# The mixture-of-experts stages: scoring from the layer's own rows, one-hots for several tiles at once, 39 tiles

## The reference, cut to what matters

```python
def _layernorm(x, axis=-1, eps=1e-05):
    m = jnp.mean(x, axis=axis, keepdims=True); v = jnp.var(x, axis=axis, keepdims=True)
    return (x - m) / jnp.sqrt(v + eps)

def _L0_ffn_ref(x, centroids, gamma, beta, W1, b1, W2, b2):      # E = 8 experts, D = 128, F = 512
    def _sublayer(xs, g, b, W1e, b1e, W2e, b2e):
        mu = jnp.mean(xs, axis=-1, keepdims=True)
        var = jnp.mean(jnp.square(xs - mu), axis=-1, keepdims=True)
        h = (xs - mu) * jax.lax.rsqrt(var + EPS) * g + b
        return xs + jax.nn.relu(h @ W1e.T + b1e) @ W2e.T + b2e
    feats = x.reshape(-1, x.shape[-1])
    expert = jnp.argmax(feats @ centroids.T, axis=1)
    alpha = jax.nn.sigmoid(jnp.sum(feats * centroids[expert], axis=-1, keepdims=True))
    ys = jax.vmap(_sublayer, in_axes=(None, 0, 0, 0, 0, 0, 0))(feats, gamma, beta, W1, b1, W2, b2)
    y = jnp.einsum('te,etd->td', jax.nn.one_hot(expert, E), ys)
    return (alpha * y + (1.0 - alpha) * feats).reshape(x.shape)

x = x + _L0_ffn_ref(_layernorm(x), ...)      # twice, an attention layer between
```

## Time and profile before

| | |
|---|---|
| time, median of 3 runs | 2809.09 us |
| profiled execution, its span | 2815.74 us, 2814.2 us |
| busy, share of the span: PE, DVE, ACT, POOL | 76%, 82%, 66%, 59% |
| first expert layer | 573 to 774 us |
| second expert layer | 1150 to 1352 us |

### The profile page before, as it was taken

The page is one execution under the profiler, slowest core; times in us unless marked ns, Lnnn a source line. Parts: engine busy times, 40 slices in busy tenths (PEclk is TensorE's granted clock), DMA queues, the critical chain, the costliest instruction groups (busy, mean ns, idle before and its releaser), DMA issues. The chain is left out here.

```text
span 2814.2 us, 59782 instructions
## 1 busy us (share of the span) xinstructions
PE 2125.2 (76%) x17516; PEld 1786.7 (63%) x17517; DVE 2299.4 (82%) x5649; ACT 1857.1 (66%) x4289; POOL 1659.4 (59%) x1493
## 2 busy tenths in 40 slices
PE   5628888867589999666458887888888537888886
PEld 2226666756578888566346665777777426777776
DVE  6489999864478888633878884999999888999997
ACT  3559999734455555244335555999888438999886
POOL 0179999615400000055456554999999418999996
PEclk9769999969799999689679997999999759999999
DMA  2013333141200000111010000000000000000001
GB/s 57 2 33 98 96 97 96 64 134 40 60 16 0 0 0 1 31 39 43 25 39 2 0 0 1 1 0 0 0 0 0 1 1 1 0 0 0 0 0 30
DMA packets 67864, 70.93 MB, mean 25 GB/s; under 512 B 10328, under 2 KB 46384, under 8 KB 67632
## 3 DMA queue, kind: packets, MB, share of 16 engines
q1 hardware_dynamic: 61488, 57.56, 7.0%
q0 software_dynamic: 5120, 10.50, 1.4%
q10 hardware_dynamic: 1120, 1.22, 0.2%
HBM read 57.45 MB, written 11.80 MB: 25 GB/s over the span
## 5 line engine op out<-in xcount | busy, mean ns | idle before, releaser
L1794 POOL TENSOR_TENSOR k7a_psums<-k7a_sims 128x1024 f32<-128x1024 f32 x224 | 421.8, 1917 | 18.0 <-DVE k7a_w L2002 13.8
L1794 POOL TENSOR_TENSOR k5a_psums<-k5a_sims 128x1024 f32<-128x1024 f32 x224 | 421.8, 1914 | 17.9 <-DVE k5a_w L2002 13.7
L957 POOL TENSOR_TENSOR mc_hc<-mc_h,mc_cs 128x512 f32<-128x512 f32 x256 | 327.7, 1298 | 32.6 <-DVE mc_h L924 16.6
L1859 PE MATMUL k7a_pw<-g_ident,k7a_w 128*128 128x128 f32 x2048 | 265.5, 277 | 72.5 <-DVE k7a_hid L2011 47.9
L1859 PE MATMUL k5a_pw<-g_ident,k5a_w 128*128 128x128 f32 x2048 | 265.5, 277 | 72.3 <-DVE k5a_hid L2011 47.9
L924 DVE TENSOR_TENSOR_SCAN mc_h<-mc_dA,mc_inj 128x512 f32<-128x512 f32 x256 | 298.2, 1199 | 4.0 <-ACT mc_dA L881 4.0
L1859 PEld LDWEIGHTS k7a_pw<-g_ident,k7a_w 128*128 128x128 f32 x2048 | 226.8, 141 | 115.7 <-DVE k7a_w L2002 52.7
L1859 PEld LDWEIGHTS k5a_pw<-g_ident,k5a_w 128*128 128x128 f32 x2048 | 226.8, 141 | 115.5 <-DVE k5a_w L2002 52.5
L2002 DVE SCALAR_TENSOR_TENSOR k7a_w<-k7a_psums,k7a_best,k7a_lift 128x1024 f32<-128x1024 f32 x224 | 279.1, 1270 | 0.5 <-ACT k7a_lift L1930 0.3
L2002 DVE SCALAR_TENSOR_TENSOR k5a_w<-k5a_psums,k5a_best,k5a_lift 128x1024 f32<-128x1024 f32 x224 | 279.1, 1270 | 0.5 <-ACT k5a_lift L1930 0.3
L1930 ACT ACTIVATE k7a_lift<-k7a_psums 128x1024 f32<-128x1024 f32 x224 | 228.4, 1019 | 35.3 <-DVE k7a_w L2002 30.9
(11 more groups left out here) (532 smaller groups left out, 6059.7 us busy)
## 6 DMA issues: line engine op xcount, KB each, us to landing
mc_cs<-c_rows SPq DMA_DIRECT2D x128, 256.0 KB, 3.1
e_w<-in_L_ffn_W_dram SPq DMA_DIRECT2D x16, 256.0 KB, 5.1
token_rows<-e_zn SPq DMA_DIRECT2D x16, 256.0 KB, 3.6
e_zn<-token_out SPq DMA_DIRECT2D x16, 256.0 KB, 5.7
g_X<-in_L_attn_a_x_dram SPq DMA_DIRECT2D x8, 256.0 KB, 6.0
out_dram<-g_X SPq DMA_DIRECT2D x1, 2048.0 KB, 8.7
e_zs<-token_rows,e_token POOLq DMA_INDIRECT x80
token_out<-e_ys,e_token POOLq DMA_INDIRECT x80
```

Source lines behind the costliest of these rows:

```text
L957: nc.gpsimd.tensor_tensor(hc[:, q % RH, :], h_[:, q % RB, :], cs[:, S % RC, :], ALU.mult).then_inc(outs, 1)
L1794: nc.gpsimd.tensor_tensor(psums[:, h - 1, :, :], rows_of(p, h), s2, ALU.add).then_inc(pooled, 1)
L1859: ins = nc.tensor.matmul(pw[:, j, :], w[:, h % WR, j * P:(j + 1) * P], env.ident[:, :], start=(h == 0 and j % 4 == 0), stop=(h == HD - 1 a ...
```

## The change

- Scales: the 17 operations run inside the layer's block. The two square roots stand on ScalarE behind its first and its second copy of transposed rows.
- Scores: TensorE transposes X, not the normalised rows, and does not wait for these; the centroids have their mean subtracted (three VectorE operations), which leaves the order of scores and, times 1/sd, the score itself. In the first layer the rows of centroids, gamma, beta and b1 are loaded, transposed and copied inside the block, ahead of the first score. SP issues these four loads and the 17 of the weights first.
- Normalising: VectorE does six chunks, GpSimd the last two. VectorE waits for the weight loads only after the list is made.
- Maxima are taken from PSUM, without a copy.
- Weight groups: two ahead of the counts (`EARLY`), seven more ahead of the list (`MIDDLE` = 9), the last seven behind it; ScalarE copies them in the same order, with its half of the one-hots in between, and its sigmoid after them.
- One-hots: the tile comparison in two halves, its scaling on ScalarE and GpSimd, half by half; the place comparison in five operations of 8, 8, 8, 4 and 4 tiles, with the places in PSUM; the products wait once for each of the five.
- The loop runs over 39 tiles.
- End: ScalarE writes two chunks to PSUM, which VectorE adds; GpSimd adds the other six; VectorE takes all statistics.

```diff
 TensorE
-                pe.wait_ge(normed, n + 1)
                 need(pe, written, n - 1)
-                    ins = nc.tensor.transpose(pz[...], zn[:, n * TPC + k, :], env.ident[:, :])
+                    ins = nc.tensor.transpose(pz[...], env.X[:, n * TPC + k, :], env.ident[:, :])
                 ins.then_inc(turned, 1)
+                if n == 1 and rows:
+                    pe.wait_ge(centred, 3)
+                    nc.tensor.transpose(counts[:, 0:3 * E], rows3[:, :], env.ident[0:3 * E, 0:3 * E])
+                    nc.tensor.transpose(counts[:, 3 * E:3 * E + E * J], rows1[:, :], ...).then_inc(rows_turned, 1)
+                    pe.wait_ge(rows_out, 2)
...
-            for g in range(EARLY, len(groups)):
+            for g in range(EARLY, min(MIDDLE, len(groups))):
                 turn_group(g)
-            pe.wait_ge(spread, 2)
-            for t in range(NT):
-                pe.wait_ge(compared, t + 1)
-                nc.tensor.matmul(ids[...], hotr[:, t, :], hotq[:, t, :, :], ...).then_inc(found, 1)
+            for i, (t0, t1) in enumerate(GROUPS):        # (0, 8), (8, 16), (16, 24), (24, 28), (28, 32)
+                pe.wait_ge(spread, 1 if t1 <= NT // 2 else 2)
+                pe.wait_ge(spread_p, 1 if t1 <= NT // 2 else 2)
+                pe.wait_ge(compared, i + 1)
+                for t in range(t0, t1):
+                    ins = nc.tensor.matmul(ids[...], hotr[:, t, :], hotq[:, t, :, :], ...)
+            ins.then_inc(found, 1)
+            for g in range(MIDDLE, len(groups)):
+                turn_group(g)
 ScalarE
                 nc.scalar.copy(zc[:, n % 2, :], pz[:, n % 2, :]).then_inc(written, 1)
+                if n < 2:
+                    act.wait_ge(scaled, (7, 13)[n])
+                    nc.scalar.activation(tmp[:, 2, :], tmp[:, 1, :], ACT.Sqrt).then_inc(rooted, 1)
+                if n == 1 and rows:
+                    act.wait_ge(rows_turned, 1)
...
+            for i, (t0, t1) in enumerate(HALVES):
+                act.wait_ge(vec, EQUAL[i])
+                nc.scalar.mul(hotq[:, t0:t1, 0, :], equal[:, t0:t1, :], env.steps[:, 2, 0:1]).then_inc(spread, 1)
+            for g in range(MIDDLE, len(groups)):
+                evacuate(g)
...
+                    dst = pz[:, SUMS.index(n), ...] if n in SUMS else own[:, t, :]      # SUMS = (3, 7)
+                    ins = nc.scalar.mul(dst, own[:, t, :], alpha[:, t:t + 1])
 GpSimd
+            pool.wait_ge(scaled, 17)
+            for n in range(OWN, NC_):                    # OWN = 6
+                nc.gpsimd.tensor_tensor(zn[:, ts, :], env.X[:, ts, :], over(env.mean[:, ts], P), ALU.subtract)...
+                nc.gpsimd.tensor_tensor(zn[:, ts, :], zn[:, ts, :], over(env.rnorm[:, ts], P), ALU.mult)...
+            for i, (t0, t1) in enumerate(HALVES):
+                pool.wait_ge(vec, EQUAL[i])
+                nc.gpsimd.tensor_tensor(hotq[:, t0:t1, 1, :], equal[:, t0:t1, :], ..., ALU.mult).then_inc(spread_p, 1)
...
-            for j in range(NJ):
+            for j in range(USED):                        # 39
...
+                    pool.wait_ge(gained, n + 1)
+                    nc.gpsimd.tensor_tensor(env.X[:, ts, :], env.X[:, ts, :], own[:, ts, :], ALU.add).then_inc(pooled, 1)
 VectorE
-            link(nc.vector.tensor_copy(sc[:, :, :], scores[:, 0:NT * E]...))
-            link(nc.vector.tensor_reduce(mx[:, :], sc[:, :, :], AX, ALU.max))
+            link(nc.vector.tensor_reduce(mx[:, :], raw_scores, AX, ALU.max))
...
+            for t0, t1 in HALVES:
+                link.inc(nc.vector.tensor_tensor(equal[:, t0:t1, :], across(env.steps[:, 0, 0:NJ], t1 - t0),
+                                                 over(block128[:, t0:t1], NJ), ALU.is_equal))
-            nc.vector.tensor_scalar(hotq[:, :, 0, :], equal[:, :, :], env.steps[:, 2, 0:1], None, ALU.mult)...
-            for t in range(NT):
-                nc.vector.tensor_scalar(hotr[:, t, :], env.steps[:, 1, :], place[:, t:t + 1], None,
+            for t0, t1 in GROUPS:
+                nc.vector.tensor_tensor(hotr[:, t0:t1, :], across(env.steps[:, 1, :], t1 - t0), over(place[:, t0:t1], P),
                                         ALU.is_equal).then_inc(compared, 1)
```

More of the change, by code:

```diff
@@ L1038, in expert_weights @@
         later += [(w1[:, e, :, :], a["W1"][e].rearrange("(j p) c -> p j c", p=P)), (w2[:, e, :], a["W2"][e])]
[L1039 to L1043, removed]
+    rows = [(rows3[0:E, :], a["centroids"]), (rows3[E:2 * E, :], a["gamma"]), (rows3[2 * E:3 * E, :], a["beta"]),
+            (rows1[:, :], a["b1"].rearrange("e (j p) -> (e j) p", p=P))]
     groups = []
@@ L1047, in expert_weights @@
                    (w2T[:, e, :], [w2[:, e, j * P:(j + 1) * P] for j in range(J)])]
-    return env.expert_weights, (fetched, later, groups, b1)
+    return env.expert_weights, (fetched, later, groups, b1, rows, rows1, rows3)
 def experts(nc, env, a, ahead, tag):
@@ L1058, in experts @@
     NJ = (NT + E - 1 + 1) // 2 * 2
[L1059 removed]
+    USED = NT + E - 1
+    assert NJ % RZ == 0 and NJ - NT == RZ and NJ <= P and USED == NJ - 1
+    OWN, SUMS = NC_ - 2, (3, NC_ - 1)
+    second_norm = (1.0, 1e-5, 0.0, 1.0)
     with ExitStack() as outer:
@@ L1062, in experts @@
         (w1T, w2T, vectors, byexpert), raw = expert_weights(nc, env, a, tag, (sb, ps, sem))
-        fetched, later, groups, b1 = raw or (None, [], [], None)
+        fetched, later, groups, b1, rows, rows1, rows3 = raw or (None, [], [], None, [], None, None)
         centT = byexpert[:, 0, :]
@@ L1090, in experts @@
             "kept", "based", "gained", "tabled"))
+        scaled, rooted, shared, centred, rows_in, rows_turned, rows_out, spread_p, pooled, tail = (sem(x) for x in (
+            "scaled", "rooted", "shared", "centred", "rowsin", "rowsturned", "rowsout", "spreadp", "pooled", "tail"))
         gathered, stored = [sem(f"gathered{z}") for z in range(RZ)], [sem(f"stored{z}") for z in range(RZ)]
@@ L1193, in body @@
             def body(it, begin, last):
-                for z in range(RZ):
-                    if not (last and z == RZ - 1):
+                for z in range(RZ - 1 if last else RZ):
+                    if not (last and z == RZ - 2):
                         turn(*after(it, z))
@@ L1202, in _ @@
             rounds(pe, NJ // RZ, body)
-            second(NJ // RZ - 1, RZ - 1)
+            second(NJ // RZ - 1, RZ - 2)
         def relu(eng, z, half):
@@ L1217, in _, with evacuate @@
         def _(act):
+            def evacuate(g):
+                act.wait_ge(placed, g + 1)
+                nc.scalar.copy(groups[g][0], turned_w[:, g % 2, :]).then_inc(evacuated, 1)
             for n in range(NC_):
@@ L1253, in body @@
                     relu(act, z, 0).then_inc(relu_a, 1)
-                    if not (last and z >= RZ - 2):
+                    if not (last and z >= RZ - 3):
                         stage(*after(*after(it, z)))
@@ L1264, in _ @@
                 act.wait_ge(loaded[n], 16)
-                for t in range(n * TPC, (n + 1) * TPC):
-                    ins = nc.scalar.mul(own[:, t, :], own[:, t, :], alpha[:, t:t + 1])
+                for k in range(TPC):
+                    t = n * TPC + k
+                    dst = pz[:, SUMS.index(n), k * P:(k + 1) * P] if n in SUMS else own[:, t, :]
+                    ins = nc.scalar.mul(dst, own[:, t, :], alpha[:, t:t + 1])
                 ins.then_inc(gained, 1)
@@ L1295, in _ @@
                 gather(j)
-            for j in range(NJ):
-                if j + LEAD < NJ:
+            for j in range(USED):
+                if j + LEAD < USED:
                     gather(j + LEAD)
                 scatter(j)
+            pool.wait_ge(based, NT)
+            for n in range(NC_):
+                if n not in SUMS:
+                    ts = slice(n * TPC, (n + 1) * TPC)
+                    pool.wait_ge(gained, n + 1)
+                    nc.gpsimd.tensor_tensor(env.X[:, ts, :], env.X[:, ts, :], own[:, ts, :], ALU.add).then_inc(pooled, 1)
         @block.vector
         def _(dve):
-            for n in range(NC_):
+            scales = Link(dve, scaled)
+            scale_rows(nc, env, dve, scales, rooted, tmp, second_norm)
+            scales.wait()
+            if rows:
+                dve.wait_ge(rows_in, 16 * len(rows))
+                centre = Link(dve, centred)
+                centre(nc.vector.tensor_reduce(csum[0:E, 0:1], rows3[0:E, :], AX, ALU.add))
+                centre(nc.vector.tensor_scalar(csum[0:E, 1:2], csum[0:E, 0:1], 1.0 / P, None, ALU.mult))
+                centre.inc(nc.vector.tensor_scalar(rows3[0:E, :], rows3[0:E, :], csum[0:E, 1:2], None, ALU.subtract))
+            for n in range(OWN):
                 for t in range(n * TPC, (n + 1) * TPC):
@@ L1378, in _ @@
             assert link.n == TOKEN
+            if rows:
+                dve.wait_ge(tabled, 2)
+                dve.wait_ge(fetched, 16 * len(later))
             def stage(it, z):
@@ L1415, in _ @@
             rounds(dve, NJ // RZ, body)
```

(21 more changed lines are left out.)

72 lines of the change are left out of this document (40 added, 32 removed).

## The result

| | before | after |
|---|---|---|
| median of the runs (four each) | 2809.61 us | 2791.39 us |
| ratio, 95% interval | | 0.9928 (0.9916 to 0.9941) |
| profiled execution, its span | 2815.74, 2814.2 | 2793.79, 2791.9 |
| first expert stage, entry to the next layer's entry | 202.27 | 195.18 |
| second expert stage | 202.87 | 192.01 |

The changed kernel is 18.2 us faster; 20.4 were forecast, and 2791.4 lies in the forecast's own range. In the two profiles the stages give 7.1 + 10.9 = 18.0; the other 4.3 us between the spans lie outside the stages, where nothing was changed.

The account below looks back on a forecast made before the run. The expert stages' head was taken as a chain with no engine full. First stage 2.8 + 1.8 + 1.7 = 6.3, second 10.6 + 1.8 + 1.7 = 14.1, together 20.4 us: 2809.09 - 20.4 = 2788.7, range 2780 to 2799.

Parts of the forecast that it names:

- Scoring starts earlier: Stage heads: TensorE transposes X itself, so the first product comes 1.0 us earlier in the first stage, 5.5 in the second.
- rival (b): Scoring runs at 2.4 GHz, so normalising sets its end: some 6 us more gain, 2782.5 us; chance 0.08.
- Between scores and comparison: Heads: the scores' copy goes, 0.46 us in both stages; fewer weight transposes ahead of the counts save perhaps 0.3 in the first.
- The one-hots: Heads: half comparisons, scaling moved off VectorE and five wide comparisons take 6.2 us instead of 10.85, 4.65 less.
- rival (a): Half the gain: VectorE stalls beside GpSimd, weight groups eat the first stage's gain, tail sums slow; 13.4 us, 2795.7; chance 0.20.
- First stage, what is late next: First stage's head: moved weight groups and ScalarE's queue hold the first tile, so it enters only 2.8 us earlier.
- the chain's 6.4: First stage's head: gain from earlier scoring, dropped copy, fewer transposes and one-hots alone, 6.4 us, the upper end.
- Rival (c): Weight groups leave TensorE at 2.4 GHz, so groups and first tile pass faster: 3.5 us more, 2785; chance 0.10.
- The loop: Dropping the always empty 40th tile saves one step at the last scatters' pace, 1.8 us a stage (1.3 to 3.3).
- The tail: Stage end: GpSimd does six sums at 1.04 us each, VectorE keeps up and ends 1.7 us earlier a stage.
- theory 1: Follow-ups' explanation, not the prediction's: GpSimd is through some 6.5 us after its last instruction, so its new tail sums delay stage ends.
- Rival (d): Slower: loops entered in another phase of TensorE's clock; with 50 further tiles at 1.2 GHz the time is 2824; chance 0.03.

Follow-up runs that it names:

- e8: Changed kernel with the 40th, empty tile back in the loop; ratio to the kernel before 0.9963, +6.7 us against the changed kernel.
- e10: Changed kernel with the places in SBUF instead of PSUM; ratio to the kernel before 0.9940.
- e11: Changed kernel with the sigmoid and its table load ahead of the last seven weight copies on ScalarE; ratio to the kernel before 0.9923.
- e6: Changed kernel with the one-hots as before (whole comparison, 32 one-tile comparisons, places in SBUF); ratio to the kernel before 0.9973, +9.6 us against the changed kernel.
- e5: The changed kernel run again, unaltered; ratio to the kernel before 0.9939; its profiled execution took over 500 us longer, so its profile is not read.
- e1: Changed kernel with the last sums of all eight chunks on VectorE, none on GpSimd; ratio to the kernel before 0.9914.
- e2: Changed kernel with GpSimd summing only the first three chunks and VectorE the other five; ratio to the kernel before 0.9921.
- e3: Changed kernel with the expert block closed without the wait for GpSimd's queue (no_gpsimd_drain); ratio to the kernel before 0.9916.
- e4: Kernel before, with one small unneeded memset on GpSimd after ScalarE's last scaling; ratio to the kernel before 1.0003.
- e12: Changed kernel with the block closed without GpSimd's wait and the sigmoid ahead of the last weight copies; ratio to the kernel before 0.9904, median 2785.41 us.
- e7: Changed kernel with TensorE again transposing normalised rows, so scoring waits for them; ratio to the kernel before 0.9987, +13.5 us against the changed kernel.

## Why the prediction was right, point by point

| term, us | forecast | measured in the profile of after |
|---|---|---|
| first stage, start of the loop | 2.8 | 6.3 (first scatter, from entry) |
| second stage, start of the loop | 10.6 | 11.5 |
| tile 40, each stage | 1.8 | 2.6 and 1.6; over all profiles 3.5 |
| tail, each stage | 1.7 | 2.0 and 1.6 |
| from VectorE's end to the next layer, each stage | none | -3.84 and -3.86 |

- **Scoring starts earlier**: right. Second stage 6.5 for 5.5, as the eight transposes took 1.44 us, not 1.9 (the first 0.5 us were still at 2.4 GHz: 1.00 over 1140.37 to 1140.90), and the 0.4 us of hand-offs did not show; first stage 0.94 for 1.0, with the square root's load behind a copy. From then on the clock stayed at 0.50, so rival (b) did not come here, but it can: in e8 the second scoring kept the 2.4 GHz of the layer before for its first 6.5 us and fell to 1.2 only then, and the first gather came 2.5 us earlier than in the profile of after. The two windows of e8, columns as in the earlier trace rows:

```profile
1146.80:1153.20 6.40, 5.54 (x46) 4.83 (x46) 3.94 (x18) 3.80 (x7) 1.27 (x4) 1.00 0.01 4
1153.30:1164.00 10.70, 10.52 (x53) 10.42 (x51) 8.64 (x25) 2.34 (x4) 3.12 (x4) 0.50 0.53 155
```

- **Between scores and comparison**: near. The comparison begins 1.84 us earlier in the first stage and 6.80 in the second, so this step gave 0.90 for 0.76 and 0.29 for 0.46.
- **The one-hots**: right, 4.70 and 4.72 for 4.65, and for the reason given: with the places in PSUM VectorE isn't held up beside GpSimd (e10). So rival (a) did not come.
- **First stage, what is late next**: this step failed. The first tile does enter behind ScalarE's queue, as the prediction says, 4.5 us earlier (2.8 forecast; the seven groups took 5.18 us for 6.2, at a clock of 0.81). But the loop does not begin with it. The first scatter follows the first gather by 11.1 to 11.6 us in both stages of before, after, e10 and e11, whether the first tile enters 3.2 or 5.9 us after that gather (12.5 in e6's first stage, at a clock of 0.58 behind the entry), and e11 moves the entry without moving the scatter. So the chain's 6.4, which the text names as the upper end, was the value to take. What takes up the difference is a wait of VectorE. In its list the first tile's result stands behind the second tile's relu, and that relu begins 10.0 to 10.5 us after the first gather in both stages of all 13 profiles (e5's apart). Where the first tile enters up to 4.9 us after the gather, VectorE has stood idle for 2.0 to 2.8 us before this relu; where it enters after 5.4 to 5.9, for 0.7 to 1.2. The relu in the second stage of after, in its first stage and in the first stage of e11 (first gathers at 1178.19, 616.09 and 617.72):

```profile
1188.30 0.61 DVE L1224 TENSOR_SCALAR e_hid<-e_ph,e_ownvectors 128x128 f32<-128x128 f32 x2 [2.71 <-PE e_ph L1190]
```
```profile
626.27 0.61 DVE L1224 TENSOR_SCALAR e_hid<-e_ph,e_ownvectors 128x128 f32<-128x128 f32 x2 [0.72 <-PE e_ph L1190]
```
```profile
627.96 0.61 DVE L1224 TENSOR_SCALAR e_hid<-e_ph,e_ownvectors 128x128 f32<-128x128 f32 x2 [2.13 <-remote]
```

  What VectorE waits for there is not settled. GpSimd's first seven gathers end 8.5 to 8.7 us after the first of them begins, just as regularly; whether they are the cause was not tried. Rival (c) came in part, for the groups alone: from the first tile's entry to the first scatter the granted clock was 0.71 after and 0.76 before.
- **The loop**: the mechanism right, the size wrong. The short steps at the end come when the gathers run out, and with 39 tiles there are as many of them: seven scatters behind the last gather in both profiles, the last three 1.7, 1.8 and 1.3 us apart (before 1.8, 1.8 and 1.3). So the tile that goes is one of the middle: 3.5 us by the two means, near the mean step of 116.6 / 38 = 3.1.
- **The tail**: right, but GpSimd's sums took 1.24 us, not 1.04, so VectorE waits 0.35 for some of them.
- **What is missing**: the prediction let the next layer follow VectorE's end. It asked what GpSimd's new sums do to VectorE, and not how late GpSimd itself may end. The gap is theory 1's 7.7 us. e1 to e4 show the cause, and e12 closes the gaps again.
- **Rival (d)** did not come: the loops are not longer.

With 3.5 for the loop and 1.8 for the tail in place of one profile's, the terms come to 7.8 and 13.0 = 20.7 us; by the three ratios the change is worth 17 to 20. The difference of up to 3.5 us stays open; single profiles differ by as much.

## What to carry to other kernels

When work is moved to an idle engine near the end of a block, ask when that engine itself is through, not only whether it keeps up: an engine that ended early had cover that the profile doesn't show. Work that is cut out of a loop is worth the loop's pace in the middle, not that of its last steps. And a total that comes out as forecast proves no term: here three were off by 3 us or more over both stages: the first loop's start, the tile and the end.

## What was not expected of the hardware

- In these blocks GpSimd, which issued 39 or 40 gathers and as many scatters, held the end for 6.4 to 6.6 us behind its last instruction, whether that was a scatter, a sum or a 0.10 us memset. In the state-space block of the same trace, where it issues no transfer, it was through 0.06 us after its last sum. That the transfers are the cause was not tried.
- Both engines pay when VectorE and GpSimd clash: comparisons 6.82 for 4.67, products 3.97 for 2.99 (e10). Two inputs in SBUF are not the only way into it: VectorE's normalising has one such tensor, and took 1.1 us instead of 0.26 for each of four rows, with GpSimd at its usual 1.04 (e7).
- The second scoring begins at 2.4 GHz and the clock then falls to 1.2 during the work: 0.6 us after the stage's entry in the profile of after, 6.5 us after it in e8, where TensorE had been busy for 5.54 of 6.40 us. It stayed there with TensorE busy for 19.57 of 19.60 us and for 10.52 of 10.70.
